# Moving one small matmul ahead of a run of three matmul groups in a six-layer attention kernel

## What is computed

```
for i in range(DEPTH):                     # 6 layers
    x = attn_layer(shift_tokens(x), Wqkv[i], q_scale[i], k_scale[i], Wo[i]) + x
    x = ffn_layer(shift_tokens(x), ln_g[i], ln_b[i], W1[i], b1[i], W2[i], b2[i]) + x

def attn_layer(...):                       # 16 heads of 64, windows of 32 that see the one before
    q, k, v = split(x @ Wqkv)              # 128 -> 3 x 1024
    q, k = l2norm, scale, rotary
    out = softmax(q k^T * 8, masked) v
    return out @ Wo

def ffn_layer(x, g, bln, W1, b1, W2, b2):  # 128 -> 2 x 341 -> 128
    xn = (x - mean) / sqrt(var + 1e-05) * g + bln
    a, gate = split(xn @ W1 + b1)
    return a * gelu(gate) @ W2 + b2
```

## Time and profile before

| | |
|---|---|
| median of 3 runs | 1648.02 us (1647.44 to 1648.67) |
| profiled execution, its own time | 1647.35 us |
| its span, first to last instruction | 1645.6 us |
| TensorE busy | 1592.4 us, 97% of the span |
| TensorE weight loads busy | 1367.4 us, 83% |
| VectorE, ScalarE, GpSimd busy | 1368.5, 1343.9, 1322.8 us (83%, 82%, 80%) |
| granted TensorE clock, mean | 0.998 of full speed |

### The profile page before, as it was taken

How to read it: one execution, slowest core, us unless ns; L and a number is a source line. 1 busy time by engine, 2 the same in 40 slices (tenths; PEclk the granted TensorE clock), 3 DMA queues, 4 the chain that set the end, 5 groups by cost and what they waited for, 6 DMA issues and landing times.

```text
span 1645.6 us, 50851 instructions
## 1 busy us (share of the span) xinstructions
PE 1592.4 (97%) x19920; PEld 1367.4 (83%) x19920; DVE 1368.5 (83%) x2011; ACT 1343.9 (82%) x2518; POOL 1322.8 (80%) x1283
## 2 busy tenths in 40 slices
PE   5899999999999999999999999999999999999997
PEld 3678888888888888888888888888888888888786
DVE  6888888888888888888888888888888888888865
ACT  5768888788888888888888888888888888878884
POOL 8988898888889888889888889878888776677742
PEclk9999999999999999999999999999999999999999
DMA  4345233433323344232344333334333332222231
GB/s 135 99 119 140 71 98 85 119 108 98 107 76 90 102 116 120 77 106 76 100 113 114 99 83 99 84 105 132 86 94 87 92 85 69 77 73 69 64 113 33
DMA packets 184871, 156.89 MB, mean 95 GB/s; under 512 B 111550, under 2 KB 156092, under 8 KB 184636
## 3 DMA queue, kind: packets, MB, share of 16 engines
q1 hardware_dynamic: 184636, 153.64, 33.4%
HBM read 27.56 MB, written 1.05 MB: 17 GB/s over the span
## 4 chain that ended last, share of the span: by engine, by line
PE 81%; DVE 7%; ACT 4%; POOL 3%; issue 3%; DMA 0%; SPq 0%; POOLq 0%; ACTq 0%; DVEq 0%
PE ps_pv L793 12%; PE ps_s L769 10%; PE ps_pv L812 9%; PE ps_tr L730 9%; PE ps_qn L702 8%; PE ps_qn L703 7%; PE ps_qn L704 7%; PE ps_tr L714 5%; PE ps_pv L802 3%; PE ps_s L752 2%; PE ps_qn L892 2%; PE ps_qn L893 2%; PE ps_qn L894 2%; DVE ss L1542 1%; POOL qk L1968 1%
## 5 line engine op out<-in xcount | busy, mean ns | idle before, releaser
L1968 POOL TENSOR_TENSOR qk<-qk,t 128x1024 f32<-128x1024 f32 x192 | 455.8, 2376 | 92.8 <-DVE qk L1532 92.6
L1529 DVE TENSOR_TENSOR t<-ps_qn,tab 128x512 f32<-128x512 f32 x384 | 264.6, 689 | 129.3 <-ACT sq L1128 116.4
L1980 POOL TENSOR_TENSOR qkr<-qk,rinv 128x1024 f32<-128x1024 f32 x192 | 361.7, 1905 | 7.7 <-POOL rinv L1960 0.4
L1115 ACT ACTIVATE pbd<-ps_tr 64x512 f32<-64x512 f32 x384 | 226.0, 589 | 63.9 <-PE ps_tr L714 60.9
L702 PE MATMUL ps_qn<-w_hi,xs_hi 128*128 128x512 f32 x576 | 260.3, 452 | 16.4 <-DVE qk L1532 7.5
L1532 DVE TENSOR_TENSOR qk<-ps_qn,tab 128x512 f32<-128x512 f32 x384 | 261.5, 681 | 0.0
L1128 ACT ACTIVATE sq<-ps_qn 128x512 f32<-128x512 f32 x384 | 228.6, 596 | 35.8 <-PE ps_qn L704 31.1
L1161 ACT ACTIVATE qbd<-ps_tr 64x512 f32<-64x512 f32 x384 | 226.8, 591 | 32.7 <-PE ps_tr L730 27.2
L703 PE MATMUL ps_qn<-w_lo,xs_hi 128*128 128x512 f32 x576 | 229.2, 398 | 0.0
L704 PE MATMUL ps_qn<-w_hi,xs_lo 128*128 128x512 f32 x576 | 228.6, 397 | 0.0
L1542 DVE TENSOR_REDUCE ss<-sq 128x32 f32<-128x2048 f32 x96 | 216.6, 2256 | 0.0
(11 more groups left out here) (168 smaller groups left out, 3206.1 us busy)
## 6 DMA issues: line engine op xcount, KB each, us to landing
v_own<-v_new SPq DMA_DIRECT2D x96, 512.0 KB, 3.2
v_back<-v_new SPq DMA_DIRECT2D x96, 384.0 KB, 3.5
v_back<-v_own SPq DMA_DIRECT2D x94, 128.0 KB, 2.3
kT<-kT SPq DMA_DIRECT2D x84, 128.0 KB, 2.7
w_raw<-in_Wqkv SPq DMA_DIRECT2D x18, 512.0 KB, 5.2
rot<-in_rot SPq DMA_DIRECT2D x48, 128.0 KB, 2.6
fx<-xmid SPq DMA_DIRECT2D x96, 64.0 KB, 2.1
xsh<-x SPq DMA_DIRECT2D x190, 32.0 KB, 2.6
```

Source lines behind the costliest of these rows:

```text
L1529: v.tensor_tensor(t2[:, part].rearrange("p (h s d) -> p h s d", s=2, d=DH // 2), swapped, tab[:, 2 * k + 1:2 * k + 2, :].rearrange("p o (s ...
L1968: g.tensor_tensor(qk[b][:, part], qk[b][:, part], t2[:, part], ALU.add).then_inc(added[b], 1)
L1980: g.tensor_tensor(qkr[b][:, part].rearrange("p (h d) -> p h d", d=DH), qk[b][:, part].rearrange("p (h d) -> p h d", d=DH), rinv[b][:, k * ...
```

## The change

In half 1 of each step TensorE issues the broadcast ahead of chunks 4 and 5 instead of behind them. In steps 0 to 39 it then stands behind the query transposes; in steps 40 to 47, where those come earlier, it stands behind up 1. Chunks 4 and 5 and up 2 follow one another with nothing in between. The other engines' lists are the same, and so is every product and every bank.

```
@@ -998,10 +998,10 @@
                         ffn_up(i, 1)
                         if rec_tile(i, b, RATES_AT) is None:
                             transpose_queries(i, b)
+                        ffn_broadcast(i)
                         qkv(i, b, (4, 5))
                         if i.n == 1:
                             transpose_pair(2)
-                        ffn_broadcast(i)
                         ffn_up(i, 2)
                     scores(i, b, 0)
                     scores(i, b, 1)
```

## The result

Side by side with the kernel before, on one chip, the changed kernel took 1659.54 us (median of 4 runs, 1658.71 to 1660.70) against 1647.73 us (4 runs, 1646.98 to 1648.67). The ratio is 1.0072, with a 95% interval of 1.006 to 1.0084: slower by 11.8 us. The forecast was 1661.7 us; the measured time lies inside its range, 1657.3 to 1665.2. The profiled execution took 1659.8 us, with a span of 1658.0. That is 12.4 more than the span before; 0.63 of it lies in the start-up, ahead of the first instruction that the change touches (TensorE's first mask product starts at 65.49 in place of 64.87 us), and 11.8 behind it.

What follows compares the result with a forecast made beforehand. TensorE's own order was taken as the bound, busy throughout an ordinary 31.72 us step. 31 x 0.44 = 13.6 us, other steps 0, on the profiled 1647.35 gave 1661.0; the median's 0.67 offset made 1661.7 us, range 1657.3 to 1665.2.

Steps and rivals of the forecast that it cites:

- A wait takes the broadcast's place: Ahead of up 2 in half 1, TensorE would wait 0.3 to 0.4 us for VectorE's copy of chunk 4.
- The faster rival: Up 2 need not wait for chunk 4's copy; one precision switch a step goes, 2.5 us less, 1645.5 us; chance 0.03.
- the main term: In 31 ordinary steps the broadcast ahead of chunk 4 costs 0.44 us each, 31.72 to 32.16 us: 13.6 us.
- TensorE's own loss: Between chunk 5 and up 2 TensorE idles about 0.37 us, and the scores start that much later.
- VectorE's chain loses all and reaches chunk 3 last: VectorE has no hole from its copies to the product chunk 3 of the next half awaits; all 0.44 us arrives.
- The rival that absorbed 0.15 us a step at chunk 3: VectorE has room; TensorE's 0.37 meets a 0.22 us wait: 0.15 x 31 = 4.7 us, 1652.7 us; chance 0.05.
- Chunk 3's wait stays: Sign at chunk 3 of the next half: its wait stays; the forecast is wrong if it shrinks.
- New layers: In the last tile of layers 0 to 4, VectorE's 0.57 us wait for ScalarE hides 0.44: cost 0.
- The dearer rival: New layers and recurrent steps pay too: 44 x 0.44 = 19.4 us, 1667.4 us; chance 0.07.
- Recurrent steps: In steps 40 to 47, the 0.63 us hole between up 1 and chunk 4 takes the broadcast's 0.44: cost 0.
- Step 3: Pipeline step with the broadcast but no up projection; it can lose 0 to 0.44 us, taken as 0.
- The precision switch and the page's rule: Between fp32 and other products a switch costs at most 0.07 us, taken as 0; back-to-back batching gains nothing at full clock.

## Why the prediction was right, and where its sizes were off

**A wait takes the broadcast's place.** Right. The wait ahead of up 2 is there in all 44 steps with an up projection, released by VectorE's copy, and none was listed before. The run ahead of up 2 cannot close up. The faster rival would have needed up 2 free of that copy, and is refuted.

**The size of the main term.** The broadcast was priced at 0.44 us, from the centring matmul; an ordinary step lost 0.39 to 0.40. The slope with more or less work is one (0.08, 0.40, 0.83), so the product does take about 0.44, and 0.04 comes back as a constant. The trace shows where. Counted back from its second pass (817.60 less the usual 0.23), chunk 4 streams from 817.37 in before, while the last query transpose starts at 817.23 and they stand 0.11 apart, so the array is free at 817.34: a hole of 0.03 to 0.04 us, where the prediction had "without a hole". Chunk 4's weights load from 817.27, right when the last load of the transposes ends. In after the broadcast's second pass starts at 825.57 and takes 0.22, and chunk 4 streams from 825.79 (826.02 less 0.23): no hole. That it is the weight load that makes the hole is argued and not shown. Over 31 steps 0.048 us less each is 1.5 of the 1.8 us between forecast and measurement.

**TensorE's own loss.** Predicted 0.37 us to the scores, measured 0.28. A copy that is 0.39 late in place of 0.44 makes 0.05 of the 0.09. It did not enter the sum, because VectorE's path lost more.

**Which path sets the end.** The step "VectorE's chain loses all and reaches chunk 3 last" held here, but its picture was incomplete. The text gave TensorE's path 0.22 us to spare at chunk 3. It has 0.00 to 0.05: it goes not only to chunk 3 directly but through the probability transposes and ScalarE's square into the same rotation of VectorE. The broadcast behind up 2 showed it (+0.32 with copies on time), and the early residual addition agrees (0.12 back in place of 0.2), though there the square is late as much by VectorE's late sums as by TensorE. In the timed change all three arrive close together; VectorE's own chain, 0.39 late, is the last. The rival that absorbed 0.15 us a step at chunk 3 rested on that same false room. "Chunk 3's wait stays" was wrong for a smaller reason: it grew from 0.22 to 0.34, as the predicted 0.37 and 0.44 themselves would have given 0.29.

**New layers.** Predicted 0, measured 0 (-0.14 us over all five). With double the broadcast they pay 0.07, so the cover is nearer 0.8 us than the 0.57 read off VectorE's wait for ScalarE. The dearer rival saw a margin of 0.13 there that was much larger.

**Recurrent steps.** Predicted 0, "give or take 0.07"; they gained 0.09 to 0.10 each. The hole between up 1 and chunk 4 took the broadcast. TensorE in such a step of the kernel after:

```profile
1351.12 0.28 PE L894 MATMUL ps_qn<-fxn_hi,w_lo 128*128 128x256 f32 x1
1351.24 0.60 PE L850 MATMUL ps_pv<-diag,ones 128*128 128x256 f32 x2
1351.87 0.47 PE L702 MATMUL ps_qn<-w_hi,xs_hi 128*128 128x512 f32 x1
```

Chunk 4 still starts 0.75 us behind up 1's last pass (before: 1338.11 and 1338.86). The copies keep their time to 0.02, and up 2 no longer stands behind the broadcast: its second pass comes 0.09 sooner and the scores 0.10. Since TensorE's path sets these steps, the 0.10 counts. I had named that margin and taken it for nothing; it is -0.7 us.

**Step 3.** It has no up projection, and I took 0 out of 0 to 0.44. It paid 0.45: nothing needed up 2 for the loss, since late copies are enough. The small terms, 0.45 - 0.14 - 0.74 and the drain's 0.11, come to -0.3 us; with the -1.5 above, the forecast's +13.6 becomes 11.8, as measured. That the small terms could be taken as nothing owes something to luck: +0.45 and -0.74 have opposite signs.

**The precision switch and the page's rule.** The step became longer with the run of three groups and no switch in it, both in the change and behind up 2. A switch itself shows no cost: the broadcast in fp32 is followed by fp32r passes in both kernels, and counted back as above these stream when it has left the array, chunk 4 from 825.79 in after and up 2 from 819.19 in before (its second pass at 819.31 less 0.12).

TensorE's busy share was to fall and did not: 1592.4 of 1645.6 us and 1607.2 of 1658.0 are both 97%. The new hole is there, but most of it is listed as busy, as seen above.

The rule on back-to-back batches of the Trainium skill, page "Perfetto Trace Analysis", section "Matmul Optimizations", had nothing to win here: the clock row was full before and is full after.

## What to carry to other kernels

A small product that needs none of the buffers its neighbours wait for may be filling a hole that no view lists as a wait; compute the releaser's end before moving it, because the hole reappears where it stood and the product is paid in full where it goes. Where the profile lists no wait, still compare ends and starts across engines: two paths that arrive within 0.05 us of each other are one bound, and a wait seen at another place (here the 0.22 us ahead of chunk 3) is no room for either. An experiment that delays each path by itself finds this, and the timed change alone does not. Here the broadcast between the v chunks delayed VectorE with TensorE on time (+0.43 us a step), and behind up 2 TensorE with VectorE's copies on time (+0.32).

## What was not expected of the hardware

- What a product cost in the queue was the time that it occupies the array less 0.04 us: about 0.12, 0.44 and 0.87 us of work ahead of chunk 4 cost 0.08, 0.40 and 0.83.
- The listed wait ahead of up 2 is 0.52 us, but TensorE's path to the scores lengthened by 0.28 only: the idle time of the weight loads begins when the last load is done, while the array is still streaming what was loaded.
- TensorE's listed busy time rose by 14.8 us with the same 19920 passes and the same clock, 0.30 of it in each ordinary step: a hole of some 0.3 us behind a run of products is mostly covered by the listed tail of its last pass (0.40 us at a spacing of 0.23). A busy share of 97% said nothing of it, before or after.
